# A graph-attention and mixture-of-experts kernel on one core: several hand-overs between the engines are moved a step apart in the main loop

## The reference, cut to what matters

```
h  = layernorm(x);  Wh = h @ W
e  = leaky_relu((Wh @ a1)[:, None] + (Wh @ a2)[None, :])
e  = where(adj > 0, e, -9e15)
x  = x + elu(softmax(e, axis=1) @ Wh)
xf = layernorm(x)
idx = argmax(xf @ router_w.T + router_b)        # one of 32 experts for each row
x  = x + relu(relu(xf @ W1[idx] + b1[idx]) @ W2[idx] + b2[idx])
```

## Time and profile before

| | before |
|---|---|
| median of 3 runs | 1376.2 us (1371.95 to 1376.54) |
| profiled execution, its own time | 1378.95 us |
| its span | 1377.4 us |
| mean granted TensorE clock | 0.822 |
| busy share of the span: PE, DVE, ACT, POOL | 67%, 64%, 53%, 45% |
| bytes moved, mean rate | 365.69 MB, 265 GB/s |

### The profile page before, as it was taken

The page is one execution under the profiler, slowest core; times in us unless marked ns, Lnnn a source line. Parts: engine busy times, 40 slices in busy tenths (PEclk is TensorE's granted clock), DMA queues, the critical chain, the costliest instruction groups (busy, mean ns, idle before and its releaser), DMA issues.

```text
span 1377.4 us, 25778 instructions
## 1 busy us (share of the span) xinstructions
PE 918.3 (67%) x3974; PEld 581.5 (42%) x4011; DVE 882.5 (64%) x4417; ACT 732.4 (53%) x1359; POOL 622.0 (45%) x650
## 2 busy tenths in 40 slices
PE   3878746677666777767677767676776664076664
PEld 2545424444444444434444434443444553054443
DVE  5777637766776676776667676666666664255553
ACT  2767745655665655555656555656554111055553
POOL 2111144555554554454554444555445762245553
PEclk9999968977998787887878787879788665599996
DMA  6999978888998888898888888889893236444442
GB/s 245 350 349 364 349 273 313 332 314 316 332 340 298 314 311 318 291 333 313 311 324 310 305 305 310 314 318 337 293 324 116 71 94 129 140 121 120 132 127 60
DMA packets 111112, 365.69 MB, mean 265 GB/s; under 512 B 28982, under 2 KB 62223, under 8 KB 78305
## 3 DMA queue, kind: packets, MB, share of 16 engines
q1 hardware_dynamic: 80610, 302.25, 61.6%
q0 software_dynamic: 28288, 61.66, 13.1%
q10 hardware_dynamic: 2176, 1.38, 0.3%
HBM read 352.06 MB, written 32.05 MB: 279 GB/s over the span
## 4 chain that ended last, share of the span: by engine, by line
PE 30%; issue 21%; DVE 19%; DMA 16%; POOL 7%; ACT 3%; DVEq 2%; POOLq 1%; another core or an unknown queue 0%; ACTq 0%; SPq 0%
PE psF L1492 18%; DMA G_all<-wh_table,idx 7%; DMA out_x<-yb,tok 6%; POOL G_all L594 4%; PE psL L1573 2%; DVE top_word L871 2%; POOL x L610 2%; PE psW L1481 2%; PE psT L1564 2%; DVE el L1122 2%; ACT sg L703 2%; ACT xT L695 1%; DVE xn L1149 1%; PE psF L1494 1%; DVE yb L1425 1%
## 5 line engine op out<-in xcount | busy, mean ns | idle before, releaser
L594 POOL DMA_INDIRECT G_all<-wh_table,idx x384 | 393.8, 1026 | 464.4 <-DVE idx L1070 229.2
L703 ACT ACTIVATE sg<-raw_all,minus_half 128x2048 fp8e4<-128x2048 int32 x256 | 504.5, 1992 | 0.0
L1492 PE MATMUL psF<-sg,fold_w 128*128 128x512 fp8e4 x1024 | 351.9, 506 | 0.8 <-DVE mean_sb L1033 0.6
L1554 PE MATMUL psO<-G_all,diag 128*128 128x256 f32 x640 | 171.7, 420 | 61.2 <-DVE diag L1105 61.2
L728 ACT ACTIVATE xT<-psT 128x256 f32<-128x256 f32 x64 | 24.5, 383 | 330.3 <-PE psT L1564 330.3
L1492 PEld LDWEIGHTS psF<-sg,fold_w 128*128 128x128 fp8e4 x1024 | 123.4, 126 | 164.5 <-issue 113.6
L1554 PEld LDWEIGHTS psO<-G_all,diag 128*128 128x128 f32 x640 | 128.3, 209 | 83.3 <-issue 65.5
L1564 PE MATMUL psT<-ident,xn 128*128 128x128 f32 x128 | 35.9, 375 | 191.4 <-DVE xn L1149 191.4
L871 DVE MAX8 top_word<-psF 128x8 f32<-128x256 f32 x256 | 107.1, 424 | 54.2 <-PE psF L1494 46.3
L657 POOL DMA_INDIRECT out_x<-yb,tok x81 | 82.6, 1020 | 86.7 <-DVE yb L1425 68.9
L1564 PEld LDWEIGHTS psT<-ident,xn 128*128 128x128 f32 x128 | 16.0, 175 | 195.6 <-issue 195.5
(11 more groups left out here) (218 smaller groups left out, 1832.2 us busy)
## 6 DMA issues: line engine op xcount, KB each, us to landing
raw_all<-in_adj SPq DMA_DIRECT2D x256, 1024.0 KB, 6.5
xb<-regions SPq DMA_DIRECT2D x84, 130.0 KB, 2.1
wh_table<-G_all POOLq DMA_DIRECT2D x8, 1040.0 KB, 9.0
w_sb<-in_x SPq DMA_DIRECT2D x8, 1024.0 KB, 7.6
xr<-in_x SPq DMA_DIRECT2D x64, 128.0 KB
G_all<-wh_table,idx POOLq DMA_INDIRECT x384
w_sb<-in_L_ffn_W SPq DMA_DIRECT2D x2, 1024.0 KB
w_sb<-in_L_ffn_W SPq DMA_DIRECT2D x4, 512.0 KB
```

The costliest lines, as they stand in the source:

```text
L594: pool.indirect_dma_start(out=G[par][:, k, :], out_offset=None, in_=table[:, :], in_offset=bass.IndirectOffsetOnAxis(ap=idx[par][:, k:k + ...
L703: act.activation(sg[par][:, q, :], raw[q], ACT.Sign, bias=minus_half[:, 0:1], saturate=False).then_inc(a_sg, 1)
L1492: pe.matmul(words, fold_w[:, j, :], sg[par][:, 2 * h:2 * h + 2, j * WORDS:(j + 1) * WORDS], start=(j == 0), stop=False)
L1554: pe.matmul(psO[par][:, 0:D], diag[:, k, :], G[par][:, k, 0:D], start=(k == 0), stop=False)
```

## The change

Nothing is computed otherwise; instructions change places in the lists of VectorE, TensorE and ScalarE. SP's and POOL's lists stay as they are.

- VectorE: `rows_of_slots(u + 1)` moves from late in step u to its head, behind `indices(u + 1)`. The whole decode, from `merge_first` to `decode_keep`, is done for strip t - 1, one step after its search. The searches move to the last third of the step. `place_logits` to `place_one_hot` move from the head of the step to behind `slots_of_rows(u + 2)`, and `post_norm` and the rest of `place_*` close the step.
- TensorE: both halves of the fold of strip t are done in step u, the first behind `tail_scores`, the second behind `tail_ends`. `logits(u - 2)` takes the place of `logits(u - 1)`. `tail_slots`, `ranks` and `post_transposes` close the step.
- ScalarE: `transposes2(u - 2)` stands near the head of step u, behind `attention_sum`; the four `signs` have no other wait between the second and the fourth.
- `search(t, 0)` gets a wait for the merge of strip t - 1. Ahead of the loop the decode of strip 7 and the fold of strip 8 are left out (they are now in step 0), and two more steps are written out instead of looped.

```diff
@@ rounds
-            peeled(max(4, NS - LAG - 2), NS - LAG)
-            loop(NS - LAG, NS - 2)
+            peeled(max(4, NS - LAG - 2), NS - LAG + 2)
+            loop(NS - LAG + 2, NS - 2)
@@ ScalarE
             def step(u, par, do):
+                if do.post:
+                    attention_sum(u - 1, 1 - par)
+                if do.place:
+                    transposes2(u - 2)
                 if do.prepare:
                     count_tail(u + 2, par)
-                if do.post:
-                    attention_sum(u - 1, 1 - par)
                 if do.ahead:
                     signs(u + LAG + 1, 1 - par, 0)
...
                     signs(u + LAG + 1, 1 - par, 1)
                     signs(u + LAG + 1, 1 - par, 2)
-                if do.post:
-                    transposes2(u - 1)
-                if do.ahead:
                     signs(u + LAG + 1, 1 - par, 3)
@@ search
                 v.wait_ge(pe_fold, t * 2 + q // 2 + 5)
+                if q == 0 and (not isinstance(t, int) or t):
+                    v.wait_ge(v_dec, t * VD - VD + 5)
@@ VectorE, the step after the change (all lines, conditions left out)
+                indices(u + 1, 1 - par)
+                rows_of_slots(u + 1, 1 - par)
+                slot_scores(u, par, half_up(u, par) * GATHERS)
+                penalties(u)
+                merge_first(t - 1)
+                merge_rest(t - 1)
+                merge_second(t - 1)
+                softmax(u, par)
+                decode_words(t - 1)
+                decode_bits(t - 1)
+                post_min(w)
+                decode_columns(t - 1)
+                decode_keys(t - 1)
+                row_weights(u, par)
+                post_elu(w)
+                decode_first(t - 1)
+                post_x1(w, ...)
+                slot_weights(u, par)
+                decode_rest(t - 1)
+                post_stats(w, 1 - par)
+                decode_second(t - 1)
+                post_mean(w, 1 - par)
+                search(t, 0)
+                post_variance(w, 1 - par, w)
+                search(t, 1)
+                decode_keep(t - 1)
+                slots_of_rows(u + 2, par)
+                place_logits(y); place_best(y); place_argmax(y); place_expert(y); place_one_hot(y)
+                search(t, 2)
+                search(t, 3)
+                post_norm(w, 1 - par)
+                place_ranks(y); place_pick(y); place_position(y, par)
@@ TensorE
-            fold(LAG, 0, 0)
...
                 if do.attend:
                     tail_scores(u, par)
                 if do.search:
-                    fold(u + LAG, par, 1)
-                if do.place:
-                    ranks(u - 2)
+                    fold(u + LAG, par, 0)
                 if do.attend:
                     tail_weights(u, par)
                     weighted_sum(u, par)
+                if do.place:
+                    logits(u - 2)
                 if do.prepare:
                     tail_ends(u + 2)
+                if do.search:
+                    fold(u + LAG, par, 1)
+                if do.prepare:
+                    tail_slots(u + 2, par)
+                if do.place:
+                    ranks(u - 2)
                 if do.post:
                     post_transposes(u - 1)
-                if do.ahead:
-                    fold(u + LAG + 1, 1 - par, 0)
-                if do.post:
-                    logits(u - 1)
-                if do.prepare:
-                    tail_slots(u + 2, par)
```

81 lines of the change are left out of this document (21 added, 60 removed).

## The result

The changed kernel took **1342.16 us** (median of 4 runs, 1338.83 to 1344.95) against 1376.37 for the kernel before beside it (4 runs): a ratio of 0.9753, interval 0.9718 to 0.9788. So it is faster by 34 us, where I had forecast 88. Its profiled execution took 1338.83 us with a span of 1337.2; the span before was 1377.4.

The account below looks back on a forecast made before the run. Bound by engines waiting for each other, 15.93 us a step. 54 searching steps at 14.3 us save 88 us from 1378.95, other stages sum to 0; less 0.2% gives 1288 us, range 1245 to 1345 (8 in 10).

Parts of the forecast that it names:

- The late sixth index: POOL's wait before the sixth gather, 4.2 us a step, said to delay unrelated work through POOL's order and to go.
- Outside these steps: Start, step 0, step 65 and steps without a search: -2, +1, +1 and unchanged; sum 0, within 3 us.
- a TensorE stuck at 1.2 GHz: Rival: folds, weighted sum and logits on one slow path, 18.6 us a step, 1520 us; chance 0.09.
- of no effect: Rival: another wait replaces each one removed, step within 0.12 us of 15.93; chance 0.09.
- T = 14.3 us: Forecast length of a searching step, the middle between 13.9 (transfers' bound) and 14.7 (mixed clock), down from 15.93.
- the ten steps without a search ... stay: Steps without a search are set by POOL's 11 us and do not change in length.
- POOL's turn: POOL's work per step from index through six gathers, `inverse_std`, norm and position to next index: 11 us, no bound.
- The path: From one `slot_scores` to the next, through weighted sum, logits, fold's second half, searches and norm: 12.6 us at 2.4 GHz.
- rival 1: The gathers bind in a two-step loop, 2T = 21.4 + L; landing L = 9 gives 15.2 us, 1337 us; chance 0.20 with its neighbouring case.
- its sign for itself: Rival 1 would show as VectorE waiting over 2 us a step at L1076.
- a step of 15.7 us: Neighbouring case of rival 1: both fold halves at the low clock nearly always, 1361 us; chance 0.20 together.
- A fourth term: VectorE's decode a step later costs nothing, filling gaps between dependent instructions; both folds in one step set the new path.

Follow-up runs that it names:

- e14: Kernel before with only the slot rows moved to the head of VectorE's step, a step ahead: 1318.54 us, ratio 0.951.
- e3: Changed kernel with logits and `tail_ends` ahead of `tail_weights` and `weighted_sum` on TensorE: 1349.09 us, ratio 0.9782.
- e7: Changed kernel with the edits of e3 and e4 together: 1358.57 us, ratio 0.9836.
- e4: Changed kernel with indices and five gathers two strips ahead on POOL, the scatter between those gathers: 1302.52 us, ratio 0.9426.
- e9: The changed kernel as it is, measured again as a control: 1290.43 us, ratio 0.9285.
- e15: e10's kernel again (slot rows and second transposes moved, rest as in the kernel before): 1271.21 us, ratio 0.9118.
- e13: The changed kernel as it is, measured a third time: 1352.13 us, ratio 0.9737.
- e10: Kernel before with only slot rows a step ahead, and second transposes' eviction and logits in the next step: 1244.76 us, ratio 0.8948.
- e17: Changed kernel with TensorE's list as in e10, VectorE's changed order kept: 1382.33 us, ratio 1.0018.
- e1: Changed kernel with `inverse_std` off POOL; VectorE copies the variance instead, inverse square root left out: 1350.82 us, ratio 0.9785.
- e5: Changed kernel with the sixth (tail) gather issued ahead of the other five: 1355.83 us.
- e6: Changed kernel without its sixth gather, so neighbours beyond the five slots of a row are left out: 1277.11 us.
- e2: Changed kernel with `inverse_std` ahead of the sixth gather on POOL: 1330.18 us in a single run.
- e18: e10's kernel a third time, as a yardstick beside e17: 1265.99 us, ratio 0.9124.
- e16: Changed kernel with the slot rows taken back behind the variance of the step, all else changed: 1366.4 us, ratio 0.9827.

## Why the prediction was right or wrong

**Right.** The direction, and where the gain came from. The late sixth index did hold up work that has nothing to do with it: moving that one call gives 68 us (e14). The start and the stage of blocks came out at a loss of 0.6 us in session 0, as in "Outside these steps" (in session 3 it is 9), and the clock in the searching steps is 0.81 (I had asked for 0.8 or more). The rivals of a TensorE stuck at 1.2 GHz and of no effect did not come.

**Wrong, in the record's session: T = 14.3 us became 14.87 (57 us saved where I had 88), and "the ten steps without a search ... stay" became -16.5 us.** Three steps of the working failed.

1. *"The ten steps without a search are set by POOL's 11 us and stay."* POOL's turn I had summed as 11 us without a wait; what sets these steps now is mostly a chain I never wrote out. A step of the kernel after, without a search (timeline):

```profile
1041.06 0.23 DVE L1064 TENSOR_SCALAR slot_s<-slot_col,G_all 128x11 f32<-128x11 f32 x1
...
1044.31 4.60 PE L1534 MATMUL psO<-G_all,diag 128*128 128x256 f32 x10 [0.37 <-DVE diag L1093]
...
1049.90 0.16 PE L1504 MATMUL psW<-tails,upto 128*128 x1
1050.62 0.16 DVE L1034 COPY tail_row<-psW 128x2 f32<-128x2 f32 x1 [4.14 <-PE psW L1504]
...
1052.89 0.41 DVE L1137 TENSOR_SCALAR xn<-x 128x256 f32<-128x256 f32 x1
...
1053.86 0.16 DVE L1175 SCALAR_TENSOR_TENSOR posu<-posf 128x1 uint32<-128x1 f32 x1
...
1055.04 0.23 DVE L1064 TENSOR_SCALAR slot_s<-slot_col,G_all 128x11 f32<-128x11 f32 x1
```

   `slots_of_rows` waits for `tail_ends`, which stands behind a weighted sum of 4.60 us at 1.2 GHz; logits, placement, norm and position stand behind it on VectorE: 13.98 us from one `slot_scores` to the next. Every kernel with the changed order of VectorE and with `tail_ends` behind the weighted sum is long here in both rhythms (12.6 to 13.7 us); every one with VectorE's old order has 11.4 to 12.1, and e3 and e7, with `tail_ends` ahead, 12.28 and 11.85. The late signal has no part in it: the median gap in these steps is 0.05 us in session 0 as in session 3. Why e4, with POOL's order turned round, has the 12.6 I can't say.

2. *The path had no term for `slots_of_rows` and placement, taken as hidden beside the second half of the fold.* They are hidden only if VectorE reaches them in time. It waits 2.1 us a step for `tail_ends`, of which the matmul's end explains the smaller part: 1.43 us is the gap between that end and L1034. No row of the kernel before could have priced it, since there `slots_of_rows` came long after. Where the gap is 0.06 us (e9), the step is 13.88. The 14.3 had lain between the two, but by a path through the folds and the clock that binds in neither.

3. *POOL's turn: "0.85 from index to first gather ... 11 us, no bound".* POOL is the bound: from the position to the first gather it is 0.84 + 1.36 = 2.20 us, because the scatter stands in front, and the position is late. In session 0 the ring of scatter, L1034 and position takes 10.3 + 4.57 = 14.87 us. In session 3 rival 1's own sum, with what was measured in the step above, gives the time: from `slot_scores` (587.11) to the end of the position (598.92) 11.8; to the first gather 2.2; six gathers (588.29 to 595.97) 7.7; landing to 601.91 5.9; 27.6 us for two steps, 13.8 each. The rival had that loop right, with 21.4 for the rest against 21.7 here, but its price was for a landing L of 9 us, and its sign for itself (a wait of over 2 us at `slot_scores`) was wrong: it is 0.8 us in session 3 and 0.2 in session 0. Where `slot_scores` did wait for the data, L is 6.0 us in the median in session 3 and 6.1 in session 0. So that its 1337 us lies near the measured 1342 is luck. (Two of its figures are off, to no effect: its path of 11.2 us adds up to 11.45 by the list of the prediction, and a step of 15.7 gives 1364 us, not 1361.)

A fourth term had the wrong sign. The prediction put the decode at nothing ("it fills gaps"), took both folds in one step as the new path, and never asked what the two easy parts would give on the old lists. Taken apart in session 4: slot rows -68 us (e14), second transposes with the logits behind them a further -47 (e15), folds with searches, placement and decode +81 (e13). The time of session 3 (1290) is close to the forecast (1288), and that too is luck: beside the kernel before of its own session it saves 99 us, not 88, and of its span, against the rows of the prediction, 110 us come off the searching steps where I had 88, less 14 for the steps without a search and 9 elsewhere.

*The clock.* I took 14.3 between 13.9 and the mixture of 14.7. e10 shows what the fold of before does once the stalls are out: 0.91 granted in the searching steps, against 0.85 for the changed kernel beside it, where TensorE does the same work (busy 516.83 / 54 = 9.6 us a step against 10.0). The Trainium skill (TensorE: Matmul & The Clock Gate, "What's actually happening") has the throttled state as the default and activity as what releases it. The rows agree as far as both levels occur; but TensorE is busy for 0.72 of the time in both kernels, so the share alone doesn't tell which clock is granted. How the work is spread may: e17, with e10's list on TensorE but 2.1 us of waiting before `tail_slots`, has 0.83. No run changes the spread alone, so that stays argued.

**Still open.** What puts a session into one rhythm or the other. It isn't the kernel file (e9, e13), it isn't the chip alone (sessions 1 and 3 ran on the same one, and e1 has the gap where e9 hasn't), and it isn't seen in the times of the kernel before (1384 to 1389 us in sessions 1 to 5; its one trace has no late update). The gains of 68 and 47 us and the loss of 81 were all taken in a session with late updates; in session 3, without them, only the pair of e9 and e10 tells the loss: 46. That in the changed kernel the late release goes with POOL's row of scatter and gathers is shown (e1, e5, e6, and e2's single run); by what way POOL holds it up is not.

## What to carry to other kernels

Move one hand-over at a time and time each: here one moved call gave 68 us, the second hand-over 47, and the rest of the bundle took 81 of these 115 back. When a wait is moved up in a list that is executed in order, write out what stands behind it (here the norm, the position, the scatter and with it the next gathers) and do so for each stage at the clock of that stage, not only for the longest one. The version to use is e10's: slot rows a step ahead and the second transposes' eviction and the logits in the next step, with folds, searches and decode as they were: 1245, 1271 and 1266 us in three sessions, 8.8% to 10.5% under the kernel before.

## What the hardware showed that I had not expected

- *A signal of TensorE can reach VectorE 1 to 2 us after its matmul has ended.* The gap is 1.43 us in the median in session 0, 1.64 in session 4, 0.06 in session 3. The ends of matmuls are modelled in these traces, so an end by itself proves little; but the waiting instruction starts 10.3 us after POOL's scatter whenever the matmul ended, and 9.1 with one gather less (e6). The record of the update stands 0.02 us before L1034's start. So it is the update that comes late and not VectorE that is slow to see it. Moving `inverse_std` in front of the last gather takes it away (0.06, e2); swapping the gathers doesn't (1.65, e5). It isn't the changed kernel's alone. Of TensorE's updates with a record between 230 and 920 us, those recorded over 0.3 us after the matmul that sends them number 46 of 192 in session 0, 75 of 191 in e15 and 73 of 189 in e18 (up to 3.4 us late), but none of 218 in the kernel before, none of 247 in e9 and none of 256 in e10; of the experiments outside session 3, e16 alone has none as well. Those traces also hold fewer records of semaphore updates: 14,468 in session 0 and 12,461 to 14,747 in sessions 1, 2, 4 and 5, against 22,119 in e9, over 22,000 in all of session 3 and 22,157 in the kernel before. The Trainium skill (NOTIFIC — the notification-queue block, "Overflow: three behaviours, one of which stalls the engine") says that the path that carries such records pushes back on its producers when it is full, and that this could throttle an engine. If so, a part of the 50 us is the profiler's own. That is only argued: no run here shows a kernel without its records.
- *The transfers' ceiling was higher than I took it.* I had 356 GB/s from the stretch of 35 to 160 us as a ceiling; e10 moves 370 over its searching steps at a share of 0.98, where its step of 13.38 us is shorter than the 13.9 that I had called the transfers' bound.
- *POOL and VectorE get in each other's way.* A gather that starts just after VectorE's `diag` (two inputs in SBUF, 128x640) has started takes 1.64 us, most others 1.00 (timeline of the kernel after):

```profile
598.80 1.00 POOL L594 DMA_INDIRECT G_all<-wh_table,idx  x1 [0.31 <-issue]
...
600.10 1.64 POOL L594 DMA_INDIRECT G_all<-wh_table,idx  x1 [0.30 <-issue]
```

```profile
600.07 0.81 DVE L1093 TENSOR_TENSOR diag<-ident,pr 128x640 f32<-128x640 f32 x1
```

  The Trainium skill (SBUF — State Buffer, "SBUF: two separate sides") calls this an exclusive lock on a shared pair of ports, held for the whole instruction. The trace agrees: this gather ends 0.86 us after `diag` does, and so do all 41 that start during one between 195 and 900 us (0.87 or 0.88 us from end to end), however long `diag` had run; 34 of them last over 1.2 us, and no other gather does.
